# Entry of the causal attention: who writes the ones, when the value pads are cleared, in which order the last codes and the split go, and ten constant products

## The reference, cut to what matters

```
# quantised attention
attn = quant_act(softmax(q @ k.T), attn_alpha, attn_zp, 8)
x = x + (attn @ v) @ quant_weight(proj_w).T + proj_b
# causal attention
qkv = x @ c_attn_w + c_attn_b
k = concat([img @ uk_w.T + uk_b, k_word]); v = concat([img @ uv_w.T + uv_b, v_word])
scores = where(causal, q @ k.T / sqrt(8), -10000) + mask
x = x + ffn((softmax(scores) @ v) @ c_proj_w + c_proj_b)
```

## Time and profile before

| | |
|---|---|
| median of 3 runs | 757.5 us |
| profiled execution | 761.09 us |
| its span | 759.3 us |
| mean granted TensorE clock | 0.834 |
| TensorE, VectorE, ScalarE, GpSimd busy | 617.3, 545.5, 501.9, 231.2 us |

### The profile page before, as it was taken

The page is one execution under the profiler, slowest core; times in us unless marked ns, Lnnn a source line. Parts: engine busy times, 40 slices in busy tenths (PEclk is TensorE's granted clock), DMA queues, the critical chain, the costliest instruction groups (busy, mean ns, idle before and its releaser), DMA issues.

```text
span 759.3 us, 13342 instructions
## 1 busy us (share of the span) xinstructions
PE 617.3 (81%) x4834; PEld 370.9 (49%) x4834; DVE 545.5 (72%) x1111; ACT 501.9 (66%) x1205; POOL 231.2 (30%) x237
## 2 busy tenths in 40 slices
PE   7679996686688998994978979869768989778986
PEld 3322223264255565672655545544447754456754
DVE  6784335746899998869688777748995656988464
ACT  5459997654477886863656756738678746867762
POOL 6030005103289896982021000000055400035420
PEclk8879997799855555666798989979999999978999
DMA  8500000000000000000000000000000000000000
GB/s 282 168 1 1 1 1 1 0 1 0 1 1 1 2 1 1 1 1 1 1 1 1 1 1 2 2 0 1 1 2 2 3 0 1 0 1 2 3 1 28
DMA packets 9204, 9.88 MB, mean 13 GB/s; under 512 B 2890, under 2 KB 7988, under 8 KB 9012
## 3 DMA queue, kind: packets, MB, share of 16 engines
q1 hardware_dynamic: 9140, 9.04, 3.7%
HBM read 8.51 MB, written 0.52 MB: 12 GB/s over the span
## 4 chain that ended last, share of the span: by engine, by line
PE 44%; DVE 36%; ACT 9%; issue 7%; POOL 3%; DMA 1%; ACTq 0%; DVEq 0%; POOLq 0%
PE ps L1708 5%; PE ps L1541 4%; PE ps L1816 4%; PE ps L1695 3%; PE ps L1836 3%; ACT arena L615 3%; PE ps L1799 3%; PE ps L1612 2%; DVE s_nmB L1187 2%; DVE s_dss L1336 2%; POOL arena L456 2%; PE ps L1584 2%; DVE s_nmx L1246 2%; PE ps L2057 2%; DVE s_nmD L1441 2%
## 5 line engine op out<-in xcount | busy, mean ns | idle before, releaser
L456 POOL TENSOR_SCALAR arena<-arena,s_rB,s_zpu 128x512 uint8<-128x512 f32 x128 | 115.9, 944 | 36.6 <-DVE s_rB L1122 35.8
L653 ACT ACTIVATE arena<-ps,s_nmB 128x512 f32<-128x512 f32 x128 | 86.6, 683 | 32.7 <-DVE s_nmB L1187 32.0
L675 ACT ACTIVATE arena<-ps,s_nmx 128x512 f32<-128x512 f32 (+3 forms) x128 | 60.7, 527 | 55.4 <-DVE s_nmx L1251 55.1
L1187 DVE TENSOR_REDUCE s_nmB<-ps 128x2 f32<-128x1024 f32 x64 | 77.5, 1217 | 8.6 <-PE ps L1695 8.3
L486 POOL COPY arena<-arena 64x512 f32<-64x512 f32 x16 | 11.6, 723 | 190.0 <-PE ps L1933 187.8
L1246 DVE TENSOR_REDUCE s_nmx<-ps 128x1 f32<-128x512 f32 (+3 forms) x128 | 56.5, 483 | 17.9 <-PE ps L1802 17.1
L615 ACT ACTIVATE arena<-ps 128x1024 f32<-128x1024 f32 x64 | 60.9, 1026 | 6.5 <-PE ps L1596 6.4
L1547 PE MATMUL ps<-ones 128*128 128x512 f16 x150 | 43.7, 442 | 23.6 <-ACT s_rn L606 3.6
L1708 PE MATMUL ps<-cst,arena 128*128 128x128 f32 x256 | 59.0, 407 | 0.5 <-ACT arena L645 0.5
L1695 PE MATMUL ps<-staged 8*128 8x512 f16 x128 | 44.9, 572 | 12.8 <-ACT arena L653 12.0
L1708 PEld LDWEIGHTS ps<-cst,arena 128*128 128x128 f32 x256 | 47.5, 213 | 13.9 <-issue 7.5
(11 more groups left out here) (355 smaller groups left out, 1519.0 us busy)
## 6 DMA issues: line engine op xcount, KB each, us to landing
w_d<-in_wqkv SPq DMA_DIRECT2D x2, 768.0 KB
vec<-in_vec SPq DMA_DIRECT2D x1, 1200.0 KB, 10.9
vec<-in_vec SPq DMA_DIRECT2D x1, 960.0 KB, 8.2
w_h<-in_w SPq DMA_DIRECT2D x2, 341.0 KB
x_tok<-in_x SPq DMA_DIRECT2D x1, 512.0 KB, 4.0
arena<-in_w_f SPq DMA_DIRECT2D x2, 256.0 KB, 7.8
rope<-in_rope SPq DMA_DIRECT2D x1, 512.0 KB, 9.4
w_do<-in_wo SPq DMA_DIRECT2D x2, 256.0 KB
```

Source lines behind the costliest of these rows:

```text
L456: nc.gpsimd.tensor_scalar(u8[:, n % 4, j // 2, :, 2 * (j % 2)], prob[:, n % 2, j * 512:j * 512 + 512], sm("rB", 8)[:, c:c + 1], sm("zpu", ...
L653: nc.scalar.activation(prob[:, n % 2, j * 512:j * 512 + 512], ps[:, j, :], ACT.Exp, bias=sm("nmB", 8)[:, c:c + 1], accum_out=sm("sumB", 8) ...
L675: nc.scalar.activation(probC[:, n % 2, at(qt):at(qt) + w], ps[:, bank, col:col + w], ACT.Exp, bias=nmx[:, TB * b + qt, h:h + 1]).then_inc( ...
L1187: free(V.tensor_reduce(sm("nmB", 8)[:, c:c + 2], ps[:, 2 * half:2 * half + 2, :], X, ALU.max, negate=True), "maxB")
```

## The change

Four edits. ScalarE writes the ones of padqC, between its last codes copies, under a semaphore of its own (onesC), and GpSimd no longer does. GpSimd clears the value pads only after the first staging copy. VectorE copies the last codes ahead of split(0, 0) rather than behind it. TensorE waits for that copy, issues ten constant products, and then goes on to wait for the parts; its wait on the clearings counts five rather than six, with one more on onesC.

```diff
@@ GpSimd
-            nc.gpsimd.memset(padqC.rearrange("p t (h s) -> p t h s", h=H)[:, :, :, 48:64], 1.0)\
-                .then_inc(sem["pads_clear"], 1)
             pool.wait_ge(sem["colsumB"], B)
+            pool.wait_ge(sem["stagedC"], 1)
             nc.gpsimd.memset(vC[:, :, :, HD + 1:32], 0.0).then_inc(sem["pads_clear"], 1)
             nc.gpsimd.memset(vC[:, :, :, HD:HD + 1], 1.0).then_inc(sem["pads_clear"], 1)
@@ ScalarE
             codes_half(B * H - 2)
+            nc.scalar.activation(padqC.rearrange("p t (h s) -> p t h s", h=H)[:, :, :, 48:64],
+                                 ones16[:, 0:16].unsqueeze(1).unsqueeze(1).to_broadcast([P, T, H, 16]), ACT.Copy)\
+                .then_inc(sem["onesC"], 1)
             codes_half(B * H - 1)
@@ VectorE
                 if n == B * H:
                     rates(n - 1)
-                if n == B * H + 2:
-                    split(0, 0)
                 if B * H <= n:
                     codes_half(n - 3)
                     if n < B * H + 2:
                         pair_c(n - B * H)
+                    else:
+                        split(0, 0)
@@ TensorE
+            pe.wait_ge(sem["ptcB1"], B * H)
+            keep_busy(10)
             parts_c(0)
             pe.wait_ge(sem["maskC"], 1)
-            pe.wait_ge(sem["pads_clear"], 6)
+            pe.wait_ge(sem["pads_clear"], 5)
+            pe.wait_ge(sem["onesC"], 1)
```

## The result

The changed kernel takes 753.42 us (median of 20 runs, 749.83 to 754.64), the kernel before 757.59 us (median of 20 runs, 750.79 to 765.51). The ratio is 0.9946, with a 95% interval from 0.9926 to 0.9966, so 2.6 to 5.6 us less. Forecast were 752.6 us and a gain of 4.9. In some of its runs the kernel before takes 764 to 766 us at a lower granted clock; the ratios leave such runs out.

The account below looks back on a forecast made before the run. VectorE's own instruction list was taken to bound the entry. Terms 1.98 + 2.09 + 0 + 0.8 = 4.9 us, off the 757.5 us median, gave 752.6 us, range 746.5 to 759.

Parts of the forecast that it names:

- Bound of the entry: From 341.11 to 352.48 us the program's end hangs on VectorE instructions one behind the other; VectorE busy 11.01 of 11.40 us.
- Parts 1 and 2: Entry casts on VectorE, no longer beside GpSimd's memsets of ones and value pads, get 1.98 and 2.09 us shorter.
- the casts were slow for another reason: Rival in the entry: ScalarE's writes, not GpSimd, held the casts; no gain, 757.5 us; within gain taken back, chance 0.15.
- the moved clearing holds the second staging copy: Rival behind the first staging copy: memset holds VectorE 2.55 us, clock costs 1.1 more, 757.1 us; within the same 0.15.
- The give-back of part 2: Moved value copy delays values_b's small products by 0.29 us (bounds 0 and 1.08), cancelling the 0.29 us L811 gets back.
- a wait for the whole copy: Port-lock rule as read: a two-input VectorE operation waits for all of value copy L476, making the sum 0.8 us smaller.
- Cover of ScalarE's write: ScalarE writes the ones in its idle time before its last codes copy: 1.89 us (upper 2.4), cost 0.
- Part 3: Last codes copied ahead of the split, so GpSimd's mask copy ends before the first cast; otherwise 0.4 us of gain lost.
- Part 4: Ten constant products on TensorE before the entry transposes take 2.4 to 4.4 us; cost to VectorE 0 to 0.1 us.
- Part 5, the clock: First heads: the products make the clock fall one head later, +0.8 us; bounds 1.1 us lost to 3.9 us saved.

Follow-up runs that it names:

- codes last: Changed kernel with the last codes again copied behind split(0, 0), the ten products kept: 756.88 us, ratio 0.9994.
- neither: Changed kernel without the ten constant products and with the last codes copied behind split(0, 0): 753.45 us, ratio 0.9953.
- ones alone: Kernel before with only one edit, ScalarE writing the ones instead of GpSimd: 758.18 us, ratio 1.0027.
- codes first alone: Kernel before with only one edit, the last codes copied ahead of split(0, 0): 758.19 us, ratio 1.0040.
- single parts: Kernel before with one edit each: ones by ScalarE (ratio 1.0027), value pads cleared late (0.9951), or last codes copied first (1.0040).

## Why the forecast was right, point by point

**Bound of the entry: right.** VectorE's list set it. In every kernel but the one with the codes last, where the transposes came late, the distance is VectorE's instructions and nothing else.

**Parts 1 and 2: right, and shown.** 1.98 + 2.09 us was the sum; the trace gives 4.35 with the 0.29 of the image scores. That the time fell by nearly the same 4.2 us is in part luck, as its interval runs from 2.6 to 5.6 and the other stages vary by more than that. Moving either memset moved the long cast to wherever the memset then lay, so it is the overlap that costs, not the place of the cast. What a single profile could not tell is how steady this is: the first cast was 2.40 us in one profile of the kernel before and 1.77 in the other, so the distance saved is 3.7 to 4.35 us. That the casts were slow for another reason is refuted. That the moved clearing holds the second staging copy did not happen: the copy takes 0.68 us. But it starts at 353.85, behind both memsets and with 0.06 us of the value copy left, so a staging copy beside the large memset was not seen. What was seen there are smaller reads of PSUM, such as the reduction of 0.69 us at 351.49, and none is longer than elsewhere.

**The give-back of part 2: smaller than taken, and not where it was put.** The value copy held not the products of values_b but the small minimum before them, 0.52 instead of 0.17 us, which is 0.35 us of waiting for the 0.29 assumed:
```profile
353.41 0.52 DVE L1253 TENSOR_TENSOR s_nmx<-s_nmx,s_nsimg 128x3 f32<-128x3 f32 x1
353.85 0.68 DVE L1237 COPY staged<-ps 128x1024 f16<-128x1024 f16 x1
```
It did not reach the heads: the second head's first exponential starts 6.75 us behind the staging copy, and 6.72 and 6.73 us in the two profiles of the kernel before. So the 0.29 us that L811 gets back are gain, and the two do not cancel as forecast.

The Trainium skill (SBUF — State Buffer, "SBUF: two separate sides") says that whichever of the two engines starts first has the port pair for its whole instruction and that the other is blocked until then. The casts agree: each ended 0.3 us behind the memset. A two-input operation was late by 0.28 to 0.35 us beside copies of 0.61 to 1.08 us. In the kernel before, L811 started at 350.52 and GpSimd's copy ended at 350.95, so it could wait for no more than was left of the copy. The rule fits that too, and my reading of it, a wait for the whole copy and 0.8 us less gain, was wrong.

**Cover of ScalarE's write: right.** 1.90 us for an estimate of 1.89; doubled, it still costs nothing.

**Part 3: the reason did not hold.** I had it save 0.4 us of waiting for the mask copy. In the three profiles with the ones on ScalarE and the codes last (codes last, neither, ones alone) the mask copy had ended 0.2 us before the first cast, and the cast took 0.43 us. In the changed kernel's first profile the copy ended 0.6 us later against the bias addition, so there a cast in that place would have met it: this saving hangs on GpSimd's lead. The swap is worth 2.0 us, but only with products behind it at 1.2 GHz.

**Part 4: right as long as part 3 stands.** Products in 2.34 us, no wait on VectorE.

**Part 5, the clock: the term did not come.** I took +0.8 us; the ratios of the kernels with and without products are the same (0.9946 and 0.9943), each good to 0.002, or 2 us, so the times alone could not tell 0.8 us from nothing. The traces can. The step that failed is that the products would buy a shorter stretch at 1.2 GHz. They moved only its start, in the changed kernel into the first head, where VectorE worked without a pause, so a faster TensorE had nothing to shorten there (2.60, 2.59 and 2.60 us to the first exponential). Its end was not theirs: 9 or 15 us behind the staging copy, in two profiles of the same kernel. The price was too small as well, since these 6 us at the low level cost 2.7 us and not 1.1. With this term at 0 the sum is 4.1 us, and 4.4 with the 0.29 of the image scores; 4.2 was measured, and the interval holds all of these.

**Still open.** The ones alone in the kernel before shortened the entry by 2.0 us and showed no gain in 12 runs (753.03 to 762.4), and the codes first alone were 0.4% slower with the same entry. In their profiles the tail is 270.8 and 268.3 us, against 266.7. The tails go with the clock, not with an edit known to touch them: 270.8 us at a mean granted clock of 0.91, 268.1 to 268.8 at 0.93, 266.4 to 266.8 at 0.94, in all fourteen profiles. The 270.8 is more than the 1.4 us by which two profiles of one kernel differed, and whether such kernels meet the long tail more often was not tested. The runs of the changed kernel spread over 4.8 us and those of the one before over 14.7. The mean clock on record with each run goes the same way: in the series beside the single parts the kernel before took 757.7 to 758.5 us at 0.836, 755.2 to 756.2 at 0.840 and 751.5 to 751.8 at 0.846 to 0.847. Why one execution gets the clock back sooner than another was not found.

## What to carry to other kernels

When several instructions of one form have very different lengths on VectorE, lay GpSimd's timeline beside them before anything else. In this kernel a memset cost nothing until it met a VectorE cast, and then the cast paid for the rest of it; move it under work that reads PSUM or waits, or give it to ScalarE where that is idle. Measure such an edit as a distance between two instructions in the trace, since here 4 us were 0.5% of the time and two profiled executions of the kernel before differed by 9.5. Constant products are only safe where something has slack for their length at 1.2 GHz (4.47 us for ten here), and useless where VectorE sets the pace.

## What the runs showed that I had not expected

- A cast that found GpSimd in a memset stayed blocked through three memsets in a row, 4.53 us, without getting its turn between them.
- GpSimd pays as well: in the kernel before its value copy started 0.08 us behind VectorE's two-input difference (L1168, 0.69 us) and took 1.08 us, in the changed kernel 0.61 us; its memset of 128 elements took 0.59 us where the held cast was still to finish, and 0.32 us otherwise.
- Ten constant products took 2.34 us in the changed kernel and 4.47 us three microseconds later in the program, after a gap of 2.67 us on TensorE, a wait for one copy of 0.69 us that stood behind split(0, 0).
- The same kernel, executed twice, got the clock of 2.4 GHz back 9 us behind the staging copy in one execution and 15 us behind it in the other, which is 2.7 us of time.
